# Two-layer tanh recurrence on one core: the second rest of the split state is computed on VectorE instead of GpSimd

## The reference

```python
def layer(x, h0, Wx, Wh, b):
    xW = jnp.einsum('ntd,dh->nth', x, Wx) + b
    def step(h_prev, xw_t):
        h_next = jnp.tanh(h_prev @ Wh + xw_t)
        return (h_next, h_next)
    _, hs = jax.lax.scan(step, h0, jnp.swapaxes(xW, 0, 1))
    return jnp.swapaxes(hs, 0, 1)

x = x + layer(x, cond_1024, L0_cond_Wx, L0_cond_Wh, L0_cond_b)
x = x + layer(x, cond_1024, L1_cond_Wx, L1_cond_Wh, L1_cond_b)
```

## Time and profile before

| what | value |
|---|---|
| median of 3 runs | 2062.76 us (2062.5 to 2063.01) |
| the profiled execution, its time | 2062.76 us |
| the profiled execution, its span | 2060.9 us |
| PE busy | 2045.6 us, 99% |
| PEld (weight loads) busy | 1864.0 us, 90% |
| DVE busy | 1750.8 us, 85% |
| ACT busy | 1280.4 us, 62% |
| POOL busy | 446.9 us, 22% |
| L180 on POOL, the second rests | 2039 instructions, 432.5 us |
| L180 on DVE, the first rests and two at the start | 2041 instructions, 357.5 us |
| granted TensorE clock | 1.0 |

### The profile page before, as it was taken

One profiled execution on the slowest core, in us unless ns is written; L12 is line 12 of the kernel. 1 busy time (PEld: TensorE's weight loads), 2 busy tenths in 40 slices (PEclk: granted clock), 3 DMA queues, 4 the chain that ended last, 5 costly groups with the idle time before them and its releaser, 6 DMA issues.

```text
span 2060.9 us, 219225 instructions
## 1 busy us (share of the span) xinstructions
PE 2045.6 (99%) x98444; PEld 1864.0 (90%) x98444; DVE 1750.8 (85%) x10243; ACT 1280.4 (62%) x6660; POOL 446.9 (22%) x2061
## 2 busy tenths in 40 slices
PE   8999999999999999999999999999999999999998
PEld 6999999999999999999999999999999999999997
DVE  5888888888888888888888888888888888888887
ACT  3666666666666666666666666666666666666664
POOL 3222222222222222222222222222222222222221
PEclk9999999999999999999999999999999999999999
DMA  3000000000000000000000000000000000000000
GB/s 108 24 27 24 28 24 27 24 27 24 28 24 27 24 27 24 28 23 28 24 27 24 27 24 27 24 27 24 27 24 27 25 26 25 26 25 26 25 26 15
DMA packets 112537, 56.35 MB, mean 27 GB/s; under 512 B 12496, under 2 KB 111072, under 8 KB 112096
## 3 DMA queue, kind: packets, MB, share of 16 engines
q1 hardware_dynamic: 111456, 53.53, 8.9%
q10 hardware_dynamic: 864, 1.18, 0.2%
q0 software_dynamic: 32, 0.02, 0.0%
HBM read 37.90 MB, written 16.78 MB: 27 GB/s over the span
## 4 chain that ended last, share of the span: by engine, by line
PE 99%; DVE 0%; DMA 0%; issue 0%; ACT 0%; SPq 0%; ACTq 0%
PE ps_rec L246 44%; PE ps_rec L263 33%; PE ps_xw L223 22%; DMA wh<-wh_in 0%; DVE zt L434 0%; DVE z L441 0%; ACT h L357 0%; SPq L189 0%; SPq L191 0%; SPq L187 0%; DVE x_out L472 0%; ACTq L58 0%
## 5 line engine op out<-in xcount | busy, mean ns | idle before, releaser
L246 PE MATMUL ps_rec<-wh,h 128*32 128x128 f32 x32912 | 1259.7, 273 | 8.1 <-ACT h L357 6.9
L357 ACT ACTIVATE h<-z 128x24 f32<-128x24 f32 (+1 forms) x4096 | 659.7, 208 | 685.9 <-DVE z L441 644.1
L263 PE MATMUL ps_rec<-wh_part,h 128*32 128x128 bf16 x48960 | 1041.4, 219 | 1.2 <-issue 1.2
L246 PEld LDWEIGHTS ps_rec<-wh,h 128*32 128x32 f32 x32912 | 878.1, 109 | 35.1 <-ACT h L357 11.3
L263 PEld LDWEIGHTS ps_rec<-wh_part,h 128*32 128x32 bf16 x48960 | 726.8, 96 | 151.3 <-issue 1.5
L180 POOL TENSOR_TENSOR h<-h 128x16 f32<-128x16 f32 x2039 | 432.5, 212 | 1602.9 <-DVE h L180 1602.9
L441 DVE TENSOR_REDUCE z<-zt 128x24 f32<-128x72 f32 (+1 forms) x4096 | 668.7, 205 | 70.2 <-DVE zt L434 0.6
L351 ACT ACTIVATE ps_rec<-ps_xw,mask 128x128 f32<-128x128 f32 x2048 | 664.1, 324 | 78.0 <-PE ps_xw L223 78.0
L434 DVE STREAM_TRANSPOSE zt<-ps_rec 128x128 f32<-128x128 f32 x2048 | 649.0, 317 | 17.8 <-PE ps_rec L263 10.4
L180 DVE TENSOR_TENSOR h<-h 128x16 f32<-128x16 f32 x2041 | 357.5, 175 | 210.4 <-ACT h L357 1.4
L223 PE MATMUL ps_xw<-wx,x_mid 128*32 128x128 f32 x8192 | 403.7, 273 | 1.6 <-issue 1.6
(11 more groups left out here) (19 smaller groups left out, 12.4 us busy)
## 6 DMA issues: line engine op xcount, KB each, us to landing
x_pe<-x_t SPq DMA_DIRECT2D x256, 64.0 KB, 2.0
x_dve<-x_t SPq DMA_DIRECT2D x256, 64.0 KB, 1.9
out_t<-x_out SPq DMA_DIRECT2D x256, 64.0 KB, 1.5
wh<-wh_in SPq DMA_DIRECT2D x1, 1024.0 KB, 4.7
wx<-wx_in SPq DMA_DIRECT2D x1, 1024.0 KB, 8.1
wx<-wx_in ACTq DMA_DIRECT2D x2, 256.0 KB, 5.5
wx<-wx_in SPq DMA_DIRECT2D x2, 256.0 KB, 5.3
wh<-wh_in SPq DMA_DIRECT2D x2, 256.0 KB, 7.1
```

What stands on the lines that cost most here:

```text
L246: mm = pe.matmul(rows(ps_rec[l][n % 2], g), h_step(l, n - 1)[:, k, :], wh[l][:, k, g * P:(g + 1) * P], start=False, stop=k == KC - 1 and n ...
L263: mm = pe.matmul(rows(ps_rec[l][n % 2], g), h_bits(l, n - 1)[:, k, :], wh_part[l][:, i, at:at + P], start=False, stop=k == KB[l] - 1 and i ...
L357: act.activation(h_of(l, n)[:, tiles, :], z[l][n % 2][:, :].rearrange("p (k b) -> p k b", k=KC)[:, tiles, :], ACT.Tanh).then_inc(h_count(l ...
```

## The change

The second rest moves from GpSimd to VectorE. GpSimd keeps the preparation of the weight parts only. On VectorE, layer 1's second rest of the slot before stands behind layer 0's transpose, and layer 0's second rest of this slot behind layer 1's transpose; both are ahead of the `lower` and `total` of the layer just transposed. The semaphores that are waited for and raised are the same.

```diff
@@ gpsimd
-            for l, n in ORDER:
-                if is_split(l, n):
-                    pool.wait_ge(rest_done[l], n + 1 if l else n + 2 - PARTED)
-                    rest(pool, l, n, 2).then_inc(split_count(l, n)[0], S4 if (l, n) == (0, PARTED - 1) else 1)
@@ vector
+            def rest_second(l, n):
+                if is_split(l, n):
+                    dve.wait_ge(rest_done[l], n + 1 if l else n + 2 - PARTED)
+                    rest(l, n, 2).then_inc(split_count(l, n)[0], S4 if (l, n) == (0, PARTED - 1) else 1)
@@ vector, slot
                 n0, n1, before = number(0, s), number(1, s), number(1, s - 1)
                 if n0 is not None:
                     turn(0, n0)
+                if before is not None:
+                    rest_second(1, before)
+                if n0 is not None:
                     lower(0, n0)
                     total(0, n0)
...
                     rest_first(0, n0)
                 if n1 is not None:
                     turn(1, n1)
+                if n0 is not None:
+                    rest_second(0, n0)
+                if n1 is not None:
                     lower(1, n1)
                     total(1, n1)
```

More of the change, by code:

```diff
@@ L175, in x_of @@
             return xs[n // S4 % 2][:, :].rearrange("p (k s b) -> p s k b", s=S4, b=B)[:, n % S4]
-        def rest(eng, l, n, part):
-            step, to, of, tiles = h_step(l, n), h_cols(n, part), h_cols(n, part - 1), slice(0, KB[l])
-            return eng.tensor_tensor(step[:, tiles, to], step[:, tiles, of], h_bits(l, n)[:, tiles, of], ALU.subtract)
         @block.sync
@@ L418, in _ @@
                     at = slice(k * D, (k + 1) * D)
-                    full, left = wh[l][:, k, :], wh_rest[l][:, at]
-                    pool.tensor_tensor(left, full, upper(full), ALU.subtract).then_inc(s_wrest[l], 1)
+                    full, rest = wh[l][:, k, :], wh_rest[l][:, at]
+                    pool.tensor_tensor(rest, full, upper(full), ALU.subtract).then_inc(s_wrest[l], 1)
                     pool.tensor_copy(wh_part[l][:, 0, at], upper(full)).then_inc(s_wpart[l], 1)
                     pool.wait_ge(s_wrest[l], k + 1)
-                    pool.tensor_copy(wh_part[l][:, 1, at], upper(left)).then_inc(s_wpart[l], 1)
-                    pool.tensor_tensor(wh_part[l][:, 2, at], left, upper(left), ALU.subtract).then_inc(s_wpart[l], 1)
-            for l, n in ORDER:
-                if is_split(l, n):
-                    pool.wait_ge(rest_done[l], n + 1 if l else n + 2 - PARTED)
-                    rest(pool, l, n, 2).then_inc(split_count(l, n)[0], S4 if (l, n) == (0, PARTED - 1) else 1)
+                    pool.tensor_copy(wh_part[l][:, 1, at], upper(rest)).then_inc(s_wpart[l], 1)
+                    pool.tensor_tensor(wh_part[l][:, 2, at], rest, upper(rest), ALU.subtract).then_inc(s_wpart[l], 1)
         @block.vector
@@ L444, in total, with rest @@
                                       AX.X, ALU.add).then_inc(z_done[l], 1)
+            def rest(l, n, part):
+                step, to, of, tiles = h_step(l, n), h_cols(n, part), h_cols(n, part - 1), slice(0, KB[l])
+                return dve.tensor_tensor(step[:, tiles, to], step[:, tiles, of], h_bits(l, n)[:, tiles, of],
+                                         ALU.subtract)
             def rest_first(l, n):
@@ L448, in rest_first @@
                     dve.wait_ge(*h_count(l, n, 0))
-                    rest(dve, l, n, 1).then_inc(rest_done[l], 1)
+                    rest(l, n, 1).then_inc(rest_done[l], 1)
+            def rest_second(l, n):
+                if is_split(l, n):
+                    dve.wait_ge(rest_done[l], n + 1 if l else n + 2 - PARTED)
+                    rest(l, n, 2).then_inc(split_count(l, n)[0], S4 if (l, n) == (0, PARTED - 1) else 1)
             def lower(l, n):
@@ L510, in _ @@
             dve.wait_ge(s_hinit, 2)
-            rest(dve, 1, -1, 1).then_inc(s_hrest, 1)
+            rest(1, -1, 1).then_inc(s_hrest, 1)
             dve.wait_ge(s_hrest, 1)
-            rest(dve, 1, -1, 2).then_inc(*split_count(1, -1))
+            rest(1, -1, 2).then_inc(*split_count(1, -1))
             for s in range(T + LAG + 1):
```

## The result

The changed kernel takes 2083.6 us (median of 5 runs, 2082.7 to 2085.1) against 2062.8: 20.8 us more, ratio 1.010 with a 95% interval of 1.0086 to 1.0115. The forecast was 2146 us. The direction and the place are as forecast; the size is a quarter of it (20.8 against 83 us).

A forecast was written before the change was run, and what follows sets the result against it. TensorE's own work was taken to fill the 0.990 us period. The new loop, 0.232 + 0.175 + 0.051 + 0.573 = 1.031, adds 0.041 over 2034 half-slots: 2062.8 + 83.4 - 0.6, so 2146 us; range from rival 1 (2062) to 2200.

The forecast's parts named there:

- What bounds the kernel, and the slack: TensorE's own matmul work fills the 0.990 us half-slot; the parts matmuls' weight load has about 0.01 us of slack.
- The loop: Transpose, second rest, other layer's parts matmuls, that layer's transpose: 1.031 us against 0.990, 0.041 us more per half-slot.
- The interval behind the transpose: On VectorE, the second rest starts 0.232 us after the transpose: its duration 0.317 less an overlap of 0.085.
- The step that failed: Duration of the second rest added on VectorE, a 128x16 tensor_tensor: 175 ns from start to result.
- The bounds of 2122 and 2203: The forecast's own range in us, for an interval of 0.22 to 0.26 behind the transpose; chance 0.58.
- rival 1: VectorE's transpose lets the rest in by 0.191 us, so the weight load is in time: 2062 us; chance 0.14.
- rival 3: The transpose's block turning is latency, not occupancy of VectorE: interval 0.21 us, time 2101 us; chance 0.17.
- What was costed at nothing: VectorE's reduces behind the second rest: the wait for the transpose's result covers the delay by 0.03 us.
- the loop through ACT: Transpose, reduces, tanh, first rest, next transpose: 0.97 us in all, below 1.031, so 0.05 of delay would cost nothing.
- The tail: Last seven steps, layer 1 alone: 0.38 us in place of 0.46 each, a gain of 0.6 us.
- Rival 2: The second rest waits for the transpose's full 0.317 us: loop 1.116, time 2319 us; chance 0.08 with anything above 0.26.
- Rival 4: The parts matmuls' arrival already sets the period and VectorE delivers 0.025 us sooner: 2011 us; chance 0.03.

## Why the prediction was right and wrong

**What bounds the kernel, and the slack: right.** The weight load could be late by about 0.01, and the 0.573 from it to the next transpose is 0.574 in the changed kernel. The runs with less work for TensorE show that its own work made the 0.990, and also that little lies between it and the next loop.

**The loop: right.** Transpose, second rest, weight load, parts matmuls, next transpose. One layer alone, the idle rest ahead, the rest behind the reduces and the shared rest each move the time by what the loop's terms say, and 96 columns take it back under TensorE's 0.990.

**The interval behind the transpose: right, 0.232 forecast, 0.240 measured.** The way of working it out, duration less an overlap of 0.085, held to within 0.008: the overlap is 0.077 with 128 columns and 0.076 with 96.

**The step that failed: "a 128x16 tensor_tensor on VectorE, 175 ns from start to result".** It took 132. I had taken the interval from one row and the duration from another and added them, as if a duration did not depend on what stands ahead. In the prediction's sum, the duration was 0.043 too long, and the others too short by 0.008 (interval), 0.002 (to the weight load) and 0.001 (to the transpose): 0.032 in all, 2034 x 0.032 = 65 us, which is the miss (2146 - 2084 = 62). The forecast's excess over TensorE's 0.990 was 0.041, no larger than the error in this one term. The bounds of 2122 and 2203 missed for the same reason: they moved the interval from 0.22 to 0.26, which holds the measured 0.240, and kept the 175 ns fixed. The wide range reached down far enough only for the sake of rival 1, in which the change is hidden. That the time lies inside it is luck.

What counts is where the rest ends: 0.372 behind the transpose's start. An end of 0.372 is also 0.197 and 175 ns. Read so, rival 3 would have been right about the engine: the turning of blocks is latency, the transpose holds VectorE for about 0.20, and the record of what follows starts late by 0.04 and is short by as much. One row speaks for it: with an idle rest behind, the transpose and the second rest together hold the engine for 0.293, which is 0.20 and 0.09, and not 0.24 and 0.09. One speaks against it: the residual sum starts 0.240 behind a transpose too, and its record of 161 to 165 is short by only 17 to 20 ns, so that read backwards from its end it would have started at 0.220 to 0.224. So this reading is argued and not shown; what is shown is where the rest ends, and that the loop needs this. Rival 3's interval of 0.21 gave 2101 us; with 0.197 its sum is 0.197 + 0.175 + 0.051 + 0.573 = 0.996, and with the measured last two terms 0.999.

An estimate by the figures of the Trainium skill (Vector Engine (DVE) Microarchitecture Reference, Measured stream behaviour) is 0.208 for 128 columns. The reading of 0.197 to 0.20 is near it, and the recorded 0.240 is not. With 0.208 in the forecast's sum the time would have been 2097 us.

**What was costed at nothing: right in result, with more cover than I gave it.** The reduces did not move. I gave them 0.03 of cover; they have 0.058 (0.351 less 0.293). With an idle rest more, a delay of 0.02 was hidden below the other loop, as the 0.97 worked out for the loop through ACT says.

**The tail: right in sign, half the size.** The transposes of layer 1's last steps come 1.92 apart, where they were 1.96:

```profile
2066.92 0.39 PEld L258 LDWEIGHTS ps_rec<-wh_part,h 128*32 128x32 bf16 x24
2066.97 0.52 PE L258 MATMUL ps_rec<-wh_part,h 128*32 128x128 bf16 x24
...
2067.53 0.32 DVE L425 STREAM_TRANSPOSE zt<-ps_rec 128x128 f32<-128x128 f32 x1 [0.56 <-PE ps_rec L258]
...
2068.40 0.39 DVE L440 TENSOR_TENSOR h<-h 128x16 f32<-128x16 f32 x2 [0.20 <-ACT h L352]
...
2069.44 0.32 DVE L425 STREAM_TRANSPOSE zt<-ps_rec 128x128 f32<-128x128 f32 x1 [0.56 <-PE ps_rec L258]
```

That is 0.3 us over seven steps in place of 0.6. The rest is ready sooner, but the whole-f32 matmuls ahead of the parts are not done: the weight load starts at 2066.92, and the first matmul behind it only at 2066.97, where the two started together before (both at 2057.13 in the step of the earlier trace rows). Here, after a wait, the second rest has 174 ns.

**Rival 1** (hidden) is out, since the time moved by 20.8 us with an interval that leaves out 1. **Rival 2** (the transpose holds VectorE to its end) is out, since the rest starts 0.08 before the transpose's result is written. **Rival 4** (faster) is out, since no run with less delay went below 2063 us except where TensorE had less to do.

## What to carry to other kernels

Where a loop has a slack of 10 ns, price an inserted instruction by when its result is there, and take start and duration from the same pair of neighbours; a duration from a row where the engine had been idle was too long here for one that followed directly, by 9 ns behind a reduce and by 43 behind a transpose. Ask of each place in an in-order queue what the next engine in the loop waits for: the same 128x16 instruction cost nothing measurable on one side of the second rest and 172 us on the other. An engine at 99% says that the margin is small, not that nothing can be lost.

## What the runs showed of the hardware

- On VectorE a 128x16 tensor_tensor is recorded with 175 ns after a wait, 165 to 167 directly behind a reduce or another tensor_tensor, 156 behind a 128x128 copy from PSUM and 132 to 133 behind a 128x128 transpose, from PSUM or from SBUF. Behind the short one, the next starts after 0.053, else after about 0.08. A 128x32 one is recorded with 181 to 182 ns behind a reduce and 161 to 165 behind a transpose.
- The record of what follows starts 0.240 behind a 128x128 transpose and 0.207 behind one of 96 columns: 1.03 ns for a column.
- A second thing to wait for in front of one VectorE instruction showed as a wait instruction of its own and put that instruction 0.07 later. The separate wait was the one for ScalarE's tanh, which had just been met: its semaphore rose at 521.40, the wait instruction stands at 521.42 and the first rest at 521.49, where it would otherwise follow 0.03 behind the tanh.
- From a result on VectorE to TensorE's weight load it was 0.053, from one on GpSimd 0.051. GpSimd's 128x16 tensor_tensor takes 212 ns, but a second one starts 0.169 behind the first.
